# A network of 16 blocks in four interleaved streams on one core: the selective-scan blocks get their decays in PSUM, C's rows from DRAM beside B's, and an earlier input projection of the next batch

## The chip, the cores and the metric

The kernel runs on 1 core of a Trainium2 chip. The metric is the device time of one launch in microseconds (us), the median of several runs of the same program.

## The reference, cut to what matters

The reference is a network of 16 blocks, one after another, on `x` of 8 batches x 256 tokens x 128 channels. Two of them are selective scans (state-space blocks): the first block (`L0_scan`) and the ninth (`L2_scan`). Each normalises its input and computes, per batch:

```
xc, z   = split(x @ W_in)              # 256 channels each; L2: causal conv of 4 taps and SiLU on xc
low,B,C = split(xc @ W_xproj)          # 64, 16 and 16 columns
delta   = softplus(low @ W_dt + b_dt)  # L0: clipped to 0.001 .. 0.1
for n in 16 states, for every channel d, along the tokens t:
    h[t] = decay_n[t] * h[t-1] + delta[t]*xc[t]*B_n[t]
           # decay_n = 1 + A[d,n]*delta (L0) or exp(A[d,n]*delta) (L2)
    y[t] += C_n[t] * h[t]
out = (y + D*xc) * silu(z) @ W_out     # L0 and L2; added to x
```

The other 14 blocks are mixtures of experts, attentions, linear attention, local layers and slot layers. The change leaves what they compute as it is.

## The kernel before, in words

**Streams.** The 8 batches are four streams of two batches. Each stream goes through the 16 blocks in order with its own scratch memory and its own two PSUM banks, called `a` and `b` (128 partitions x 512 f32 each). Stream i begins when stream i-1 has added the result of its first batch of the first block to x (`added`, batch 0), so the streams are in different blocks most of the time and share the five engines.

**How the order of work is set.** Every block (`Part`) writes one generator for each engine: `pe`, `act`, `dve`, `pool`, `sp`. `Core.run` (L513) steps through all generators when the program is built, takes for each engine the piece that by its own list of instruction costs can start first, and emits it. The chip executes that fixed order: an instruction whose semaphore isn't there yet holds up everything behind it on its engine. ScalarE's table loads (L362) are put in by this planner, which lets a function that needs another table wait up to `PATIENCE` = 500 ns longer (L358). Extra matmuls that only keep TensorE's clock up are emitted where a block names a free bank (L533); the scan's inner loop names none.

**The scan block, class `Scan` (L711).** For a batch `bt`:

- TensorE projects the normalised input into bank `a` (`in`, L753). This waits for the skip term of the batch before (`skip`, L751), and in program order it stands behind the output projection (L783) of that batch, which waits for `gated` (L781). ScalarE copies it into `xc` (L803); in L2 a convolution on VectorE (L872) and a SiLU come in between. The convolution writes `h[0]`, which also holds `y`.
- TensorE computes `low` into bank `a` (L759) and B and C, in three copies, into bank `b` (L762). ScalarE copies B out (`b_rows`, L805), then `low` (L806), then a bf16 part of B and C (L807). VectorE forms two more bf16 parts with two subtractions and two casts (`split_dve`, L699, called at L841). Only then (L766) TensorE may overwrite bank `b` with the `dt` projection (L768).
- softplus runs as ScalarE, VectorE, ScalarE, ScalarE, VectorE (L810 to L846); `dx = delta * xc` (L851) ends this prologue.
- B goes to DRAM (`b_out`), and SP loads it back, broadcast to 128 partitions, three states at a time, into two ring buffers (L902): 6 transfers per batch, 5 of 384 KB and one of 128 KB. Batch by batch there are 2 x 4 x 2 = 16 passes over the loop below, 8 in each scan block.

The inner loop over the 16 states `n` has these steps:

1. ScalarE writes `decay[n % 2]` in SBUF, two activations of 128x255 (L824), two states ahead at most (L821). The first columns stay 0.0, from a memset per block (L837).
2. GpSimd (POOL) computes `h[n % 3] = dx * B_n` (`bx`, L900), both inputs in SBUF. It needs the rows of B, and the state n-3 accumulated (L897).
3. VectorE runs the scan over `decay` and `h`, both in SBUF (L857; traced as L405).
4. TensorE spreads C_n over the partitions into bank `b` (`spread`, L773) as a bf16 matmul of K=96.
5. VectorE multiplies h by C_n, which it reads from PSUM (`cmul`, L860).
6. TensorE adds h to bank `a` by a matmul with the identity (`acc`, L776).

After state 15 come the skip term (L863), the gate with `silu(z)` (L867), the output projection (L783) and the addition to x (L870).

Helpers record most instructions under one line: L326 is a matmul, L370 an activation, L392 a VectorE `tensor_tensor`, L397 `tensor_scalar`, L401 `scalar_tensor_tensor`, L405 the scan, L410 a copy or cast, L426 a memset, L460 a GpSimd `tensor_tensor`, L466 an indirect DMA, L480 a DMA from SP.

## Time and profile before

| | us |
|---|---|
| median of 3 runs | 3739.61 |
| the runs | 3732.49, 3739.61, 3739.84 |
| the profiled execution, time | 3741.74 |
| the profiled execution, span of the core | 3740.4 |
| TensorE busy in the span | 3130.3 |
| VectorE busy | 2584.6 |
| ScalarE busy | 2196.5 |
| GpSimd busy | 1512.7 |

The profile is of one execution, 1.3 us longer than its span. A busy engine is one that executes an instruction; a VectorE or GpSimd instruction that is held up after it has started counts as busy and shows a longer duration. The scan blocks lie in two stretches: the first from 48 us to some 450 us, with a remainder until 600 us, the second from 2050 us to 2650 us.

### The profile page before, as it was taken

The numbers are of one execution on the slowest core, as the hardware profiler recorded it, in microseconds if no ns is written. First come the engines' busy times: TensorE is split into PE (matmuls) and PEld (weight loads), VectorE is DVE, ScalarE is ACT, GpSimd is POOL, SyncE is SP. The second block draws the span as 40 slices with busy tenths as digits, with TensorE's granted clock in tenths as the row PEclk, the third lists the DMA queues.
The fourth block names the chain that finished last, engine by engine and source line by source line (L and its number), as shares of the span: only waits on it lengthen the run. The fifth ranks groups of instructions, "written<-read, shape, count | busy, mean of one in ns | idle before, by whom it ended". The sixth has DMA issues, their size and how long they took to land.

```text
span 3740.4 us, 53498 instructions
## 1 busy us (share of the span) xinstructions
PE 3130.3 (84%) x18885; PEld 1842.4 (49%) x19000; DVE 2584.6 (69%) x6180; ACT 2196.5 (59%) x4819; POOL 1512.7 (40%) x1308
## 2 busy tenths in 40 slices
PE   3677697989889999889899877879888888889866
PEld 1244284747544555445555433547465756534422
DVE  3879977474888777667777889976654455556522
ACT  2444445243565777567677664856486756767633
POOL 2545555443455553214655665663303321112100
PEclk9789999999999999999999988999999999999855
DMA  5122142223100010220100011344423543232110
GB/s 210 44 78 65 45 128 76 77 59 90 56 23 1 1 31 8 73 50 14 49 1 10 15 37 36 106 115 122 110 67 106 157 134 92 62 83 51 36 25 5
DMA packets 193604, 238.34 MB, mean 64 GB/s; under 512 B 36984, under 2 KB 154168, under 8 KB 191288
## 3 DMA queue, kind: packets, MB, share of 16 engines
q1 hardware_dynamic: 169016, 157.43, 14.9%
q0 software_dynamic: 24320, 77.47, 6.8%
q8 instruction: 151, 2.47, 0.3%
q14 instruction: 117, 0.96, 0.1%
HBM read 183.61 MB, written 53.74 MB: 63 GB/s over the span
## 4 chain that ended last, share of the span: by engine, by line
PE 35%; DVE 15%; ACT 11%; POOL 5%; issue 4%; SPq 2%; DMA 1%; DVEq 0%; POOLq 0%; ACTq 0%
PE psum L326 31%; ACT scratch L370 7%; DVE scratch L392 6%; PE psum L342 4%; POOL scratch L460 3%; ACT L362 3%; DVE scratch L414 3%; DVE scratch L405 2%; SPq L480 2%; DVE scratch L410 1%; DVE scratch L397 1%; DVE scratch L401 1%; POOL scratch L466 1%; DVE scratch L418 1%; ACT w_early L370 1%
## 5 line engine op out<-in xcount | busy, mean ns | idle before, releaser
L370 ACT ACTIVATE scratch<-psum 128x512 f32<-128x512 f32 (+7 forms) x1812 | 842.7, 494 | 804.2 <-PE psum L326 643.5
L326 PE MATMUL psum<-scratch 128*128 128x128 f32 (+16 forms) x8016 | 935.2, 323 | 123.2 <-ACT scratch L370 40.2
L460 POOL TENSOR_TENSOR scratch<-scratch 128x512 f32<-128x512 f32 (+3 forms) x536 | 706.3, 1331 | 668.5 <-PE psum L326 228.1
L370 ACT ACTIVATE scratch<-scratch 128x255 f32<-128x255 f32 (+11 forms) x1368 | 623.5, 480 | 552.6 <-DVE scratch L405 246.7
L326 PEld LDWEIGHTS psum<-scratch 128*32 128x32 f32 (+9 forms) x8016 | 592.6, 147 | 478.6 <-issue 212.0
L326 PE MATMUL psum<-scratch,w_constants 128*128 128x512 f32 (+2 forms) x848 | 454.7, 630 | 25.7 <-ACT scratch L370 18.8
L362 ACT ACT_TABLE_LOAD x333 | 427.2, 1283 | 31.8 <-PE psum L326 15.0
L405 DVE TENSOR_TENSOR_SCAN scratch<-scratch 128x512 f32<-128x512 f32 x256 | 420.5, 1644 | 16.6 <-POOL scratch L460 13.9
L392 DVE TENSOR_TENSOR scratch<-scratch,psum 128x512 f32<-128x512 f32 (+2 forms) x532 | 309.0, 586 | 138.6 <-PE psum L326 94.7
L342 PE MATMUL psum<-w_constants,scratch 128*128 128x128 f32 (+3 forms) x1880 | 326.2, 294 | 85.8 <-POOL scratch L460 37.2
L326 PE MATMUL psum<-scratch,w_early 128*128 128x512 f32 (+12 forms) x912 | 297.7, 466 | 74.4 <-DVE scratch L392 47.8
L414 DVE TENSOR_REDUCE scratch<-psum 128x2 f32<-128x512 f32 (+2 forms) x336 | 224.6, 676 | 162.5 <-PE psum L326 160.0
L342 PEld LDWEIGHTS psum<-w_constants,scratch 128*128 128x128 f32 (+3 forms) x1880 | 222.6, 144 | 219.1 <-issue 69.7
L392 DVE TENSOR_TENSOR scratch<-psum,scratch 128x512 f32<-128x512 f32 (+4 forms) x456 | 213.1, 474 | 125.0 <-ACT scratch L370 93.5
L466 POOL DMA_INDIRECT scratch<-L_experts_rows_dram,scratch x112 | 119.8, 1070 | 418.6 <-PE psum L326 304.0
L326 PE MATMUL psum<-w_local,scratch 128*128 128x512 f32 (+3 forms) x608 | 257.1, 529 | 20.6 <-DVE scratch L410 10.2
L326 PE MATMUL psum<-scratch,w_local 128*128 128x128 f32 (+6 forms) x1064 | 261.7, 378 | 12.7 <-ACT scratch L370 5.2
L460 POOL TENSOR_TENSOR scratch<-scratch,xpos 128x512 f32<-128x512 f32 x128 | 175.3, 1373 | 209.2 <-DVE scratch L392 207.1
L392 DVE TENSOR_TENSOR scratch<-scratch 128x32 f32<-128x32 f32 (+12 forms) x488 | 212.9, 442 | 61.4 <-ACT scratch L370 51.1
L326 PE MATMUL psum<-scratch,bf_masks 96*128 96x256 bf16 (+4 forms) x480 | 120.2, 286 | 136.4 <-DVE scratch L392 127.0
L326 PEld LDWEIGHTS psum<-scratch,w_early 128*128 128x128 f32 (+6 forms) x912 | 131.3, 180 | 196.4 <-DVE scratch L392 79.7
L460 POOL TENSOR_TENSOR scratch<-scratch,bf_masks 128x512 f32<-128x512 f32 x64 | 76.0, 1189 | 357.8 <-ACT scratch L370 357.5
(106 smaller groups left out, 4219.9 us busy)
## 6 DMA issues: line engine op xcount, KB each, us to landing
scratch<-b_out SPq DMA_DIRECT2D x80, 384.0 KB
slots_out<-scratch SPq DMA_DIRECT2D x112, 128.0 KB, 2.4
q_stack<-scratch SPq DMA_DIRECT2D x72, 192.0 KB, 2.8
scratch<-q_out SPq DMA_DIRECT2D x96, 96.0 KB
scratch<-slots_in SPq DMA_DIRECT2D x16, 512.0 KB
q_out<-scratch SPq DMA_DIRECT2D x40, 192.0 KB, 2.9
scratch<-slots_in SPq DMA_DIRECT2D x16, 448.0 KB
scratch<-q_stack SPq DMA_DIRECT2D x24, 288.0 KB
```

Of the source, the lines that this page charges most:

```text
L326: return self.engine.matmul(out, lhsT, rhs, start=start, stop=stop, **kw)
L342: return self.engine.transpose(out, src, ident)
L362: self.engine.add_instruction(mybir.InstLoadActFuncSet(name=self.nc.get_next_instruction_name(), act_func_set_id=self.table))
L370: return self.engine.activation(out, src, function, **kw)
L392: return self.engine.tensor_tensor(out, a, b, op)
L397: return self.engine.tensor_scalar(out, src, *args)
L401: return self.engine.scalar_tensor_tensor(out, a, scalar, b, *args)
L405: return self.engine.tensor_tensor_scan(out, a, b, *args)
L414: return self.engine.tensor_reduce(out, src, axis, op, **kw)
L460: return self.engine.tensor_tensor(out, a, b, op)
L466: return self.engine.indirect_dma_start(out, out_offset, src, in_offset)
L480: return self.engine.dma_start(out, src)
```

## The change

In both scan blocks:

- The decays go to PSUM bank `b`, as one buffer where there were two in SBUF. Decay n now waits for the scan of state n-1. The two zeros in front (one per half) are written by a small activation per batch; the memsets go.
- C isn't spread by TensorE any more. B and C are written to DRAM together, interleaved by state, and loaded back as two rows per state (B_n, C_n) of 256 KB each time, in four ring buffers: 16 transfers per batch. A buffer is refilled after `cmul` of the state that used it; the third load of a batch waits for `dt`. `cmul` reads C_n from the ring, in SBUF.
- The three copies of B and C, their three bf16 parts, and the four VectorE instructions for them go. `low`, B and C come from one product of 96 columns (two matmuls), copied out by one activation; the `dt` projection waits for that copy alone.
- The input projection of batch 1 (and in L2 its convolution, which now writes `h[2]`) is begun behind the skip term of batch 0, ahead of the output projection.

The attention block's `maxes` semaphores are renamed; nothing else of it changes.

```diff
-    return {"w_in": p[w_in], "w_rank": k_tiles(p[w_xproj][:, :p[w_dt].shape[0]]),
-            "w_bc": k_tiles(np.tile(p[w_xproj][:, p[w_dt].shape[0]:], (1, 3))), "w_dt": p[w_dt], "b_dt": as_cols(p[b_dt]),
+    rank = p[w_dt].shape[0]
+    low, b, c = np.split(p[w_xproj], [rank, (rank + p[w_xproj].shape[1]) // 2], axis=1)
+    b_and_c = np.stack([b, c], 2).reshape(b.shape[0], -1)
+    return {"w_in": p[w_in], "w_x": k_tiles(np.concatenate([low, b_and_c], 1)), "w_dt": p[w_dt], "b_dt": as_cols(p[b_dt]),
...
-        end, self.used = self.used, mark
-        self.b_rows = self.take(T, parts=N)
         self.used = mark
-        rings = [self.take(self.READ, T)]
-        assert self.used >= end
-        self.decay, self.h = ([self.take(D, T) for _ in range(n)] for n in (2, 3))
-        mark = self.used
-        self.low, self.rest = self.take(T, parts=self.rank), self.take(T)
-        self.used = mark
-        self.rings = rings + [self.take(self.READ, T)]
-        self.bc = self.take_bf16(T, parts=3 * 2 * N)
+        self.rings = [self.take(2, T) for _ in range(self.RINGS)]
+        end, self.used = self.used, mark + 4 * T
+        self.low_bc = self.take(T, parts=self.rank + 2 * N)
+        self.low, self.b_and_c = self.low_bc[0:self.rank], self.low_bc[self.rank:]
+        self.used = end
+        self.h = [self.take(D, T) for _ in range(3)]
         self.A = self.take(D, N)
         self.A2, self.B2 = v2(self.a, T), v2(self.b, T)
+        self.decay = self.B2
...
-            e.wait_ge(*(yield self["normed", "x"] if bt == 0 else self["skip", bt - 1]))
+            if bt == 0:
+                e.wait_ge(*(yield self["normed", "x"]))
+                self.pe_in(e, bt)
+            e.wait_ge(*(yield self["xc", bt]))
             for d in range(D):
-                last = e.matmul(self.A2[:, d, :], w["w_in"][:, d * P:(d + 1) * P], xb)
-            last.then_inc(*self.post("in", bt))
-            e.wait_ge(*(yield self["xc", bt]))
+                last = e.matmul(self.a[0:self.rank + 2 * N, 0:T], w["w_x"][:, d * (rank + 2 * N):(d + 1) * (rank + 2 * N)], self.xc[:, d, :],
+                                start=(d == 0), stop=(d == D - 1))
+            last.then_inc(*self.post("low_bc", bt))
+            e.wait_ge(*(yield self["low", bt]))
             if bt:
                 e.wait_ge(*(yield self["added", bt - 1]))
             for d in range(D):
-                e.matmul(self.a[0:rank, 0:T], w["w_rank"][:, d * rank:(d + 1) * rank], self.xc[:, d, :],
-                         start=(d == 0), stop=(d == D - 1))
-            for d in range(D):
-                last = e.matmul(self.b[0:6 * N, 0:T], w["w_bc"][:, d * 6 * N:(d + 1) * 6 * N], self.xc[:, d, :],
-                                start=(d == 0), stop=(d == D - 1))
-            last.then_inc(*self.post("rank_bc", bt))
-            e.wait_ge(*(yield self["low", bt]))
-            e.wait_ge(*(yield self["parts", bt]))
-            for d in range(D):
                 last = e.matmul(self.B2[:, d, :], w["w_dt"][:, d * P:(d + 1) * P], self.low)
             last.then_inc(*self.post("dt", bt))
-            for n in range(N + 1):
-                if n < N:
-                    e.wait_ge(*(yield self["softplus", "delta_raw", bt] if n == 0 else self["cmul", bt, n - 1]))
-                    e.matmul(self.b[:, 0:T], over(self.m["row_of_32"][:, N + n:N + n + 1], [6 * N, P]), self.bc).then_inc(*self.post("spread", bt, n))
-                if n:
-                    e.wait_ge(*(yield self["cmul", bt, n - 1]))
-                    e.matmul(self.a, self.c["ident"], self.h[(n - 1) % 3].rearrange("p a b -> p (a b)"), start=(n == 1),
-                             stop=(n == N)).then_inc(*self.post("acc", bt, n - 1))
+            for n in range(N):
+                e.wait_ge(*(yield self["cmul", bt, n]))
+                e.matmul(self.a, self.c["ident"], self.h[n % 3].rearrange("p a b -> p (a b)"), start=(n == 0),
+                         stop=(n == N - 1)).then_inc(*self.post("acc", bt, n))
...
+            if bt + 1 < PER_STREAM:
+                e.wait_ge(*(yield self["skip", bt]))
+                self.pe_in(e, bt + 1)
...
-            e.wait_ge(*(yield self["rank_bc", bt]))
-            e.activation(self.b_rows, self.b[0:N, 0:T], ACT.Copy).then_inc(*self.post("b_rows", bt))
-            e.activation(self.low, self.a[0:self.rank, 0:T], ACT.Copy).then_inc(*self.post("low", bt))
-            yield from split_act(self, e, bt, self["rank_bc", bt], self.b[0:6 * N, 0:T], self.bc)
+            e.wait_ge(*(yield self["low_bc", bt]))
+            e.activation(self.low_bc, self.a[0:self.rank + 2 * N, 0:T], ACT.Copy).then_inc(*self.post("low", bt))
...
-            if bt == 0:
-                e.wait_ge(*(yield self["zeroed"]))
+            e.activation(self.decay[:, :, 0:1], self.delta[:, :, 0:1], ACT.Copy, scale=0.0)
             for n in range(N):
-                if n >= 2:
-                    e.wait_ge(*(yield self["scanned", bt, n - 2]))
+                if n:
+                    e.wait_ge(*(yield self["scanned", bt, n - 1]))
                 yield None, ACT.Exp if self.a_is_exp else ACT.Identity
                 for d in range(D):
-                    last = e.activation(self.decay[n % 2][:, d, 1:T], self.delta[:, d, 1:T],
+                    last = e.activation(self.decay[:, d, 1:T], self.delta[:, d, 1:T],
...
-        for a in self.decay:
-            last = e.memset(a, 0.0)
-        last.then_inc(*self.post("zeroed"))
         for bt in range(PER_STREAM):
-            if self.conv:
+            if self.conv and bt == 0:
                 yield from self.convolve(e, bt)
-            yield from split_dve(self, e, bt, self.b[0:6 * N, 0:T], self.bc, self.rest)
...
-                flat, a = h.rearrange("p a b -> p (a b)"), self.decay[n % 2].rearrange("p a b -> p (a b)")
+                flat, r = h.rearrange("p a b -> p (a b)"), n % self.RINGS
                 e.wait_ge(*(yield self["decay", bt, n]))
                 e.wait_ge(*(yield self["bx", bt, n]))
-                e.tensor_tensor_scan(flat, a, flat, 0.0, ALU.mult, ALU.add).then_inc(*self.post("scanned", bt, n))
+                e.tensor_tensor_scan(flat, self.b, flat, 0.0, ALU.mult, ALU.add).then_inc(*self.post("scanned", bt, n))
                 e.wait_ge(*(yield self["scanned", bt, n]))
-                e.wait_ge(*(yield self["spread", bt, n]))
-                e.tensor_tensor(h, h, over(self.B2[:, 0:1, :], [P, D, T]), ALU.mult).then_inc(*self.post("cmul", bt, n))
+                e.wait_ge(*(yield self["rows", r, bt, n]))
+                e.tensor_tensor(h, h, over(self.rings[r][:, 1:2, :], [P, D, T]), ALU.mult).then_inc(*self.post("cmul", bt, n))
...
+            if self.conv and bt + 1 < PER_STREAM:
+                yield from self.convolve(e, bt + 1)
...
-                r, i = divmod(n, self.READ)
-                e.wait_ge(*(yield self["rows", r % 2, bt, r]))
+                r = n % self.RINGS
+                e.wait_ge(*(yield self["rows", r, bt, n]))
...
-            rows = self.s.b_out[bt]
-            e.wait_ge(*(yield self["b_rows", bt]))
-            e.dma_start(rows, self.b_rows).then_inc(*self.post_dma("written", bt, "b"))
-            e.wait_ge(*(yield self["written", bt, "b"]))
-            for r in range(-(-self.N // self.READ)):
-                first = r * self.READ
-                count = min(self.READ, self.N - first)
-                if r >= 2:
-                    e.wait_ge(*(yield self["bx", bt, first - self.READ - 1]))
-                elif r:
+            rows = self.s.b_and_c_out[bt]
+            e.wait_ge(*(yield self["low", bt]))
+            e.dma_start(rows, self.b_and_c).then_inc(*self.post_dma("written", bt, "b_and_c"))
+            e.wait_ge(*(yield self["written", bt, "b_and_c"]))
+            for n in range(self.N):
+                if n >= self.RINGS:
+                    e.wait_ge(*(yield self["cmul", bt, n - self.RINGS]))
+                elif n == 2:
                     e.wait_ge(*(yield self["dt", bt]))
-                src = rows[first:first + count].unsqueeze(0).broadcast_to([P, count, TOKENS])
-                e.dma_start(self.rings[r % 2][:, 0:count], src).then_inc(*self.post_dma("rows", r % 2, bt, r))
+                src = rows[2 * n:2 * (n + 1)].unsqueeze(0).broadcast_to([P, 2, TOKENS])
+                e.dma_start(self.rings[n % self.RINGS], src).then_inc(*self.post_dma("rows", n % self.RINGS, bt, n))
```

## Rows read from the trace of the kernel before

**Rows 1.** The page: span, and busy time of each engine.

```profile
span 3740.4 us, 53498 instructions
PE 3130.3 (84%) x18885; PEld 1842.4 (49%) x19000; DVE 2584.6 (69%) x6180; ACT 2196.5 (59%) x4819; POOL 1512.7 (40%) x1308
```

**Rows 2.** Busy time by stretch: stretch, length, then each engine, TensorE's granted clock, DMA share, GB/s.

```profile
48.00:450.00 402.00, 281.13 (x959) 132.26 (x968) 343.12 (x491) 179.75 (x366) 208.93 (x140) 0.89 0.17 55
450.00:600.00 150.00, 139.00 (x847) 101.44 (x850) 112.54 (x177) 67.15 (x118) 87.74 (x78) 0.96 0.34 102
2050.00:2650.00 600.00, 483.49 (x2372) 281.87 (x2387) 512.28 (x911) 382.87 (x796) 353.74 (x256) 0.92 0.25 72
```

**Rows 3.** The same for 50 us of the first stretch.

```profile
150.00:200.00 50.00, 33.81 (x73) 10.81 (x72) 49.47 (x48) 19.58 (x43) 41.05 (x22) 0.81 0.11 34
```

**Rows 4.** The timeline of the state loop of one stream: start, duration.

```profile
162.00 1.64 DVE L405 TENSOR_TENSOR_SCAN scratch<-scratch 128x512 f32<-128x512 f32 x1
163.56 0.65 DVE L392 TENSOR_TENSOR scratch<-scratch,psum 128x512 f32<-128x512 f32 x1
164.14 1.65 DVE L405 TENSOR_TENSOR_SCAN scratch<-scratch 128x512 f32<-128x512 f32 x1
163.67 0.91 ACT L370 ACTIVATE scratch<-scratch 128x255 f32<-128x255 f32 x2 [1.24 <-DVE scratch L405]
148.43 33.46 POOL L460 TENSOR_TENSOR scratch<-scratch 128x512 f32<-128x512 f32 x16
```

**Rows 5.** VectorE's groups by form, 48 to 450 us: count, busy us, mean ns.

```profile
L405 DVE TENSOR_TENSOR_SCAN scratch<-scratch 128x512 f32<-128x512 f32 x107 | 180.8, 1691 | 3.8 <-POOL scratch L460 3.8
L401 DVE SCALAR_TENSOR_TENSOR scratch<-scratch 128x512 f32<-128x512 f32 x14 | 13.6, 968 | 12.2 <-ACT scratch L370 12.2
L392 DVE TENSOR_TENSOR scratch<-scratch 128x512 f32<-128x512 f32 x15 | 12.2, 812 | 2.1 <-ACT scratch L370 1.9
```

**Rows 6.** The same from 2050 to 2650 us.

```profile
L405 DVE TENSOR_TENSOR_SCAN scratch<-scratch 128x512 f32<-128x512 f32 x128 | 203.2, 1588 | 11.0 <-POOL scratch L460 8.3 <-ACT scratch L370 2.7
L401 DVE SCALAR_TENSOR_TENSOR scratch<-scratch 128x512 f32<-128x512 f32 x15 | 12.3, 822 | 7.0 <-ACT scratch L370 6.9
L392 DVE TENSOR_TENSOR scratch<-scratch 128x512 f32<-128x512 f32 x19 | 17.1, 898 | 2.1 <-ACT scratch L370 2.0
```

**Rows 7.** All scans by operands, the whole span: durations min/median/max in ns.

```profile
L405 DVE TENSOR_TENSOR_SCAN scratch<-scratch x256: 1204/1384/7142, 66.6 to 2644.6; 128x512 f32<-128x512 f32 x128
L405 DVE TENSOR_TENSOR_SCAN scratch<-psum,scratch x64: 652/668/691, 787.2 to 1195.9; 128x256 f32<-128x256 f32 x64
```

**Rows 8.** The timeline of the first batch's prologue.

```profile
48.91 1.03 DVE L426 MEMSET scratch<- 128x512 f32 x2 [0.17 <-DVE scratch L392]
51.61 3.92 PE L326 MATMUL psum<-scratch,w_early 128*64 128x256 f32 x8 [0.75 <-ACT scratch L370]
55.57 0.90 ACT L370 ACTIVATE scratch<-psum 16x256 f32<-16x256 f32 x3 [4.01 <-PE psum L326]
56.50 0.42 DVE L392 TENSOR_TENSOR scratch<-psum,scratch 64x256 f32<-64x256 f32 x1 [6.56 <-ACT scratch L370]
57.72 0.28 DVE L410 CAST scratch<-scratch 32x256 bf16<-32x256 f32 x1
66.61 2.20 DVE L405 TENSOR_TENSOR_SCAN scratch<-scratch 128x512 f32<-128x512 f32 x1 [1.51 <-POOL scratch L460]
```

**Rows 9.** TensorE's spreading matmuls, the whole span.

```profile
L326 PE MATMUL psum<-scratch,bf_masks 96*128 96x256 bf16 x256 | 78.3, 307 | 104.3 <-DVE scratch L392 102.1 <-ACT scratch L370 1.3
```

**Rows 10.** ScalarE, 2050 to 2650 us by form, and its timeline at 2602 us.

```profile
L362 ACT ACT_TABLE_LOAD x80 | 102.6, 1283 | 8.1 <-PE psum L326 3.3 <-DVE scratch L405 2.7 <-DVE scratch L392 0.8
2602.94 1.69 ACT L370 ACTIVATE scratch<-scratch 128x255 f32<-128x255 f32 x4
```

**Rows 11.** DMA issues: count, KB each, median us to landing.

```profile
scratch<-b_out SPq DMA_DIRECT2D x80, 384.0 KB
slots_out<-scratch SPq DMA_DIRECT2D x112, 128.0 KB, 2.4
```

21 lines of the change are left out of this document (12 added, 9 removed).

## The prediction

> **What bounds the kernel now.** I read the page first. TensorE is busy for 84% of the span, VectorE for 69% [rows 1], but these are averages over sixteen blocks, and the change touches two. So the next view is busy time by stretch. In the first scan stretch (48 to 450 us) VectorE is busy for 343 of 402 us and TensorE for 281; in the second (2050 to 2650 us) it is 512 and 483 of 600 [rows 2]. VectorE comes first in both, and from 150 to 200 us it is busy for 49.5 of 50 us while TensorE has 33.8 [rows 3]. There the kernel waits for VectorE.
>
> The timeline shows what it does there. Scans start at 162.00 and 164.14: one state takes 2.14 us, a scan of 1.64 and a multiplication by C of 0.65, starts overlapping a little [rows 4]. An undisturbed scan takes 1.21 us (minimum 1204 ns), but the mean of all 128 in the second stretch is 1.588 and of 107 in the first 1.691 [rows 5 to 7]. GpSimd's bx goes on at the same time, 16 in 33.46 us or 2.09 each [rows 4]. The scan and bx both take two inputs from SBUF and hold each other up. The multiplication has one input in PSUM and stays at 0.65. The scans of the GLA block, 256 columns with their first operand in PSUM, are 652 to 691 ns in all 64 cases [rows 7]: never held up, and PSUM costs them nothing, as 256 columns more at the difference (1204 - 652) would give the same 1.2 us.
>
> **The change part by part**, against the profiled execution's 3741.7 us, which is 2.1 us above the median of the runs.
>
> *Decays in PSUM, C in SBUF.* The two VectorE instructions of a state change places. The scan loses its hold-up: 107 x (1.691 - 1.21) = 51 us in the first stretch, 128 x (1.588 - 1.21) = 48 us in the second. The multiplication now has two SBUF inputs. Its nearest rows are VectorE's other instructions of 512 columns with both inputs in SBUF, in the same stretches: 29 that take 25.8 us, 0.89 each, and 34 that take 29.4 us, 0.865 each [rows 5, 6]. Against 0.66 undisturbed, that is 0.23 and 0.20 more: 107 x 0.23 = 25 us and 128 x 0.20 = 26 us. The bounds are nothing (bx fits beside a scan of 1.2 us) and the scan's own 0.48 and 0.38 (51 and 48 us, all given back). I take the rows: VectorE gains 26 and 22 us. The Trainium skill ("SBUF — State Buffer", Who interferes with whom) says that a VectorE instruction with two SBUF inputs contends with a GpSimd instruction that reads SBUF, and that the later one blocks fully; one with a single SBUF input does not. That speaks for the scan and against the multiplication. Rows 5 to 7 agree with both halves.
>
> *No parts, no memsets.* The four VectorE instructions of the split run from 56.50 to 58.00 [rows 8]: 1.5 us, 8 batches per block, 12 us in each. The memsets are 1.03 us in each of 4 streams, 4 us per block. VectorE's sum: 26 + 12 + 4 = 42 us in the first stretch, 22 + 12 + 4 = 38 us in the second.
>
> *The prologue.* Eight matmul instructions of 3.92 us for low, B and C become four, 2.0 us less; three copies of 0.90 us become one, about 0.5 less; the split's 1.5 us go from the chain ahead of dt [rows 8]. That is 4 us from each batch's chain. The early input projection takes the gate, the output projection and their handovers from between the two batches of a stream, some 2 us, 8 times (an estimate; no row of mine has that chain).
>
> *Spreading.* 256 matmuls of 0.307 us go, 78 us of TensorE [rows 9]. TensorE mostly waits for VectorE in the loop, so I count them only from 450 to 600 us, where it is busy for 139 of 150 us [rows 2]: some 22 of the states, with their weight loads some 5 us. Elsewhere they are covered by VectorE; if that cover went, they would be a gain.
>
> *One decay buffer.* Now the decay of n+1 begins when scan n ends and its two activations take 0.91 us [rows 4]. The chain of a stream on its own is scan 1.21, decay 0.91, two handovers of some 0.04: 2.2 us per state, against 2.14 now. So **where one stream scans alone, nothing is gained in the loop**; the multiplication and any hold-up of it lie beside the decay. The gain needs a second stream or other work for VectorE in that gap. No row has an activation that writes PSUM; I take the 0.45 us that one takes now. The low bound is 0.30, a copy out of PSUM (three in 0.90 [rows 8]); as far upwards is 0.60; the ends move the chain by 0.3 us per state. The activation for the zeros, one per batch, costs at most another 0.45 each, 7 us of ScalarE beside VectorE's work.
>
> *Transfers.* B's rows, 80 x 384 KB and 16 smaller ones, become 256 of 256 KB: 64 MB for 32 [rows 11]. In the first stretch DMA runs at 0.17 of its capacity with 55 GB/s [rows 2], so twice the rows fit. SP issues 160 more and waits for the multiplication of n-4. A refill then has until bx of n: about three periods, 6.4 us, less the 1.3 us of bx. 128 KB land in 2.4 us [rows 11]; for 256 KB I estimate 3.2. Covered by 2 us, unless SP stands at another block's wait.
>
> **The sum.** A stretch does not shrink by all that VectorE is spared, since single-stream phases don't. I take half: 21 us in the first, plus 6 us for the first batch of stream 0 and the shorter handover to the next stream (nothing covers these), 27 us. In the second 19 us, less 8 us for ScalarE, see below: 11 us. With 5 us between: 27 + 11 + 5 = 43 us. 3741.7 - 43 = 3699, and 3697 against the median.
>
> **The rivals.**
>
> *B, the hold-ups vanish (20%).* If bx starts when a multiplication ends, its undisturbed 1.1 us fit into the scan's 1.2, and nothing waits. Then VectorE also keeps the 25 + 26 us. The full saving is 42 + 38 + 51 = 131 us; with three quarters on the path 98 us, 3642. For it: in a dense run GpSimd is always queued up behind VectorE [rows 4]. Against it: bx often comes late, released by the accumulation.
>
> *C, the wait moves (13%).* The multiplication inherits the scan's whole hold-up and single streams run at 2.2 us per state. Only the splits and memsets are left, 2 x 16 us, half of them covered, and the first batch's 6 us, against my 8 us for ScalarE and 0.06 us for each of some 120 states: 3741.7 - (16 + 6 - 8 - 7) = 3735, 3733 against the median, within 8.
>
> *D, slower by table loads (12%).* In the second stretch the decays are exponentials between other blocks' functions: 80 table loads there, 1.28 us each [rows 10]. Now two states' decays go out together, 4 activations in 1.69 us [rows 10], under one load. With one buffer that can't be; each state needs ScalarE anew. Every visit that is parted costs two loads, 2.57 us, on the chain scan, decay, scan. It decides above 17 such visits, 43 / 2.57. With 30 parted it costs 77 us against the 51 that I have without my allowance of 8: 3741.7 - 51 + 77 = 3768, 3766 against the median. For it: ScalarE is busy for 383 of 600 us there. Against it: in the first block the decay is no table function, and most decays go out singly already. The Trainium skill ("ScalarE: Activation LUTs", What ACT_TABLE_LOAD costs) adds a drain of about 1.38 us to each load. By that the 30 visits would cost 160 us and the time would be 3851; but in this trace the next activation stands right behind the 1.28 us, so the row decides.
>
> *E, late rows (4%).* If SP, in its fixed order, is held by another block in one load out of four, some 60 waits of 1 us bring 3697 + 60 = 3757.
>
> *F, the scan is held up all the same (3%).* The scan's second input and its output are in SBUF; were that enough, only the multiplication's 51 us would come on top: 3741.7 - 43 + 51 = 3750, 3748 against the median. The 64 scans of GLA speak against it.
>
> **How the numbers follow.** The forecast case has 48%, 3655 to 3722 by its bounds (half of VectorE's saving more or less). With B, C, D, E and F that is 100%. The range reaches down through most of B, to 3625, and up through C to 3748; D, most of E and F, and the tail of B, lie outside. A measurement of this kernel can tell about 0.2%, 7.5 us, from no change. Faster: 46% of the forecast, 20% of B, 6% of C: 0.72. Same: 2% of the forecast, 5% of C, 2% of F: 0.09. Slower: D, E, 2% of C, 1% of F: 0.19. The order in which the program is built shifts in all blocks, which alone can move the time by some us either way; the range has room for that.
>
> **What would show it.** The scans from PSUM at 1.21 us, none above 1.3; the multiplication at 0.80 to 0.95 on average (B: under 0.72, C: above 1.0); VectorE busy for some 80 to 90 us less over the span; TensorE for some 100 less; the dense run at 2.2 us per state with VectorE waiting for ScalarE. Stream 1's first projection some 6 us earlier. In the second stretch ScalarE's table loads at 80 to 90 (D: over 110). No wait of GpSimd for rows longer than 1 us in sum per batch. I am wrong if the first stretch doesn't end 20 us earlier, or if scans of over 1.3 us remain.

## The result, and the profile after the change

The changed kernel takes 3699.6 us (median of 4 runs, 3692.0 to 3705.2) against 3739.7 us (4 runs, 3732.5 to 3747.5): a ratio of 0.9892, with a 95% interval of 0.9867 to 0.9916. The forecast was 3697 us. The profiled execution took 3695.5 us, 1.3 us beyond its span. The page of the kernel after, span and busy time [rows 1]:

```profile
span 3694.2 us, 53129 instructions
PE 3122.3 (85%) x18672; PEld 1841.3 (50%) x18672; DVE 2531.0 (69%) x6100; ACT 2211.5 (60%) x4826; POOL 1438.5 (39%) x1308
```

VectorE is busy for 54 us less, TensorE for only 8 us less. The sum of my forecast was nearly right, so the interesting question is whether the 40 us come from where it put them. First the instructions themselves. VectorE's scan and multiplication in the kernel after, from 48 to 450 us and then from 2050 to 2650 us, by form [rows 5, 6]; the third group of the second fence is the decays, now written to PSUM, the fourth the table loads [rows 10]:

```profile
L406 DVE TENSOR_TENSOR_SCAN scratch<-psum,scratch 128x512 f32<-128x512 f32 x112 | 135.3, 1212 | 13.4 <-POOL scratch L461 10.7 <-ACT psum L371 2.2
L393 DVE TENSOR_TENSOR scratch<-scratch 128x512 f32<-128x512 f32 x128 | 126.8, 996 | 3.3 <-ACT scratch L371 2.2
```

```profile
L406 DVE TENSOR_TENSOR_SCAN scratch<-psum,scratch 128x512 f32<-128x512 f32 x123 | 148.7, 1211 | 29.6 <-ACT psum L371 18.6 <-POOL scratch L461 10.9
L393 DVE TENSOR_TENSOR scratch<-scratch 128x512 f32<-128x512 f32 x140 | 132.7, 952 | 3.7 <-ACT scratch L371 2.8
L371 ACT ACTIVATE psum<-scratch 128x255 f32<-128x255 f32 x246 | 106.7, 467 | 108.6 <-DVE scratch L406 105.4 <-PE psum L327 2.6
L363 ACT ACT_TABLE_LOAD x67 | 86.0, 1283 | 5.5 <-PE psum L327 2.5 <-DVE scratch L406 1.9
```

The scan fell from 1691 and 1588 ns to 1212 and 1211 ns; its slowest case, next fence, is 1226 ns. The multiplication, 0.65 us before, is now 0.95 to 1.0 us (its group holds 16 or 17 others too, of dx and of the gate). The hold-up has changed its instruction, and about a third of it is gone.

Over the whole span the account reads: the scans took 256 x 1.644 = 420.5 us and now take 309.4, 111 less. The multiplications between SBUF tiles were 60 with 47.5 us and are 316 with 296.9 us; what was added is 249.4 us for 256, or 0.974 each, where the PSUM form took 0.67, so 78 us come back. That leaves 33 us, and the splits (64 instructions, 28.4 us) and memsets (7.8) make it 70. The 54 that the page shows are 16 fewer. Most of that lies in instructions that the change leaves alone and that have two SBUF inputs, 11 us more in sum: the 128 of another block that read `xpos` took 115.1 us and take 123.2.

Next, all scans by operands in the kernel after (durations min/median/max in ns, first and last start), up to 700 us and from 2000 us:

```profile
L406 DVE TENSOR_TENSOR_SCAN scratch<-psum,scratch x128: 1185/1210/1225, 62.4 to 516.8; 128x512 f32<-128x512 f32 x128
L406 DVE TENSOR_TENSOR_SCAN scratch<-psum,scratch x128: 1172/1210/1226, 2070.0 to 2665.5; 128x512 f32<-128x512 f32 x128
```

and the same two of the kernel before:

```profile
L405 DVE TENSOR_TENSOR_SCAN scratch<-scratch x128: 1204/1506/7142, 66.6 to 592.5; 128x512 f32<-128x512 f32 x128
L405 DVE TENSOR_TENSOR_SCAN scratch<-scratch x128: 1204/1237/5492, 2055.2 to 2644.6; 128x512 f32<-128x512 f32 x128
```

The last scan of the first block starts 76 us earlier (592.5 to 516.8). The last scan of the second block starts 21 us *later*, and its first already 15 us later. So by 2055 us the lead is gone. Two weight loads, which can only go out once all four streams have left the seventh and the eleventh block, mark the slowest stream's way. SyncE's issues in the kernel before, then after (start us, us):

```profile
1823.36 0.38 SPq L480 DMA_DIRECT2D w_experts<-L_experts_dram  x1
3075.45 0.44 SPq L480 DMA_DIRECT2D w_early<-L_slots_dram  x1
```

```profile
1843.75 0.38 SPq L481 DMA_DIRECT2D w_experts<-L_experts_dram  x1
3071.11 0.37 SPq L481 DMA_DIRECT2D w_early<-L_slots_dram  x1
```

The slowest stream is 20 us *behind* its own time of before at 1823 us, 21 us behind at the end of the second scan block, 4 us ahead at 3075 us, and 46 us ahead at the end. Where does a lead of 76 us go? Busy time by stretch, before and then after (columns as in [rows 2]):

```profile
2650.00:3740.40 1090.40, 904.00 (x6574) 539.67 (x6634) 560.74 (x1656) 678.45 (x1228) 200.20 (x191) 0.88 0.29 77
```

```profile
600.00:2050.00 1450.00, 1299.19 (x7874) 772.38 (x7875) 1017.17 (x2778) 864.48 (x2250) 632.31 (x611) 0.95 0.13 37
2650.00:3694.20 1044.20, 902.27 (x6711) 550.40 (x6711) 567.12 (x1658) 699.18 (x1261) 217.42 (x206) 0.92 0.31 83
```

From 600 to 2050 us TensorE is busy for 1299 of 1450 us, 90%: a block that arrives early there may have to wait for TensorE instead. Its granted clock in this stretch is 0.95; in the kernel before it was 0.97. And behind 2650 us both kernels have about the same work, 904 and 902 us of TensorE by the records (60 of the kernel before's matmuls have none there, 6574 to 6634 weight loads), but the kernel after does it in 1044 us and the one before in 1090. The 46 us by which the spans differ all appear in a part without a scan block. Counted from the last scan, the kernel after makes up 67 us there (21 behind, 46 ahead): 25 of them by 3071 us and 42 behind it.

What differs at the end is how the four streams come in. SyncE's writes of the output, kernel before and then kernel after (start us, us from there to the end of the last, count):

```profile
3511.19 0.38 SPq L480 DMA_DIRECT2D out_dram<-x  x1
3545.81 47.77 SPq L480 DMA_DIRECT2D out_dram<-x  x2
3737.90 0.38 SPq L480 DMA_DIRECT2D out_dram<-x  x1
```

```profile
3488.82 39.21 SPq L481 DMA_DIRECT2D out_dram<-x  x2
3650.76 41.34 SPq L481 DMA_DIRECT2D out_dram<-x  x2
```

Before, three streams are done by 3593.6 and the fourth works alone for 144 us; after, the last one is alone for 41 us. The last 240 us of before have a mean granted clock of 0.64, the last 194 us of after 0.77:

```profile
3500.00:3740.40 240.40, 167.05 (x801) 76.40 (x810) 80.40 (x247) 90.80 (x169) 23.07 (x20) 0.64 0.10 23
```

```profile
3500.00:3694.20 194.20, 150.79 (x853) 69.53 (x850) 80.17 (x242) 91.05 (x177) 27.86 (x23) 0.77 0.12 27
```

So the traces alone offer two theories. **Theory 1**: the scans became cheaper by their place, and the end is earlier because of it. **Theory 2**: the instruction changes bring little, and the order that the planner happened to write for the last blocks brings the rest. The experiments take the instructions first, then the order. They ran on other chips, on which the kernel before takes 3829 to 3844 us, 2.4 to 2.8% more than above; comparisons below are therefore within one chip, or between two on which the kernel before takes the same time.

### The profile page after: what moved, and what is told of

It is laid out like the page before. It is cut to its first block and busy times, and to the rows that moved or that the text cites. A ratio compares the mean times of both kernels' runs of the same rounds, so it can differ in the third digit from the quotient of the medians.

```text
span 3694.2 us, 53129 instructions
## 1 busy us (share of the span) xinstructions
PE 3122.3 (85%) x18672; PEld 1841.3 (50%) x18672; DVE 2531.0 (69%) x6100; ACT 2211.5 (60%) x4826; POOL 1438.5 (39%) x1308
## 5 line engine op out<-in xcount | busy, mean ns | idle before, releaser
L371 ACT ACTIVATE scratch<-psum 128x512 f32<-128x512 f32 (+5 forms) x1780 | 834.0, 496 | 800.8 <-PE psum L327 659.7
L327 PE MATMUL psum<-scratch 128*32 128x128 f32 (+14 forms) x8016 | 941.5, 322 | 105.8 <-ACT scratch L371 39.3
L461 POOL TENSOR_TENSOR scratch<-scratch 128x512 f32<-128x512 f32 (+3 forms) x536 | 641.6, 1209 | 699.3 <-DVE scratch L423 240.8
L371 ACT ACTIVATE scratch<-scratch 128x512 f32<-128x512 f32 (+8 forms) x856 | 396.3, 469 | 228.5 <-DVE scratch L393 142.9
L393 DVE TENSOR_TENSOR scratch<-scratch 128x512 f32<-128x512 f32 (+11 forms) x728 | 448.4, 622 | 68.8 <-ACT scratch L371 56.1
L343 PE MATMUL psum<-w_constants,scratch 128*128 128x128 f32 (+2 forms) x1880 | 329.8, 297 | 77.0 <-POOL scratch L461 45.4
L371 ACT ACTIVATE psum<-scratch 128x255 f32<-128x255 f32 (+1 forms) x528 | 224.0, 458 | 272.8 <-DVE scratch L406 258.9
L406 DVE TENSOR_TENSOR_SCAN scratch<-psum,scratch 128x512 f32<-128x512 f32 (+1 forms) x320 | 349.6, 1104 | 50.9 <-ACT psum L371 23.2
L343 PEld LDWEIGHTS psum<-w_constants,scratch 128*128 128x128 f32 (+2 forms) x1880 | 226.8, 146 | 211.2 <-issue 69.3
L327 PE MATMUL psum<-scratch,w_early 128*128 128x512 f32 (+10 forms) x848 | 279.8, 465 | 61.7 <-DVE scratch L393 45.2
L327 PE MATMUL psum<-scratch,w_local 128*128 128x128 f32 (+5 forms) x1064 | 265.8, 385 | 7.7 <-ACT scratch L371 5.5
```

Source lines behind the costliest of these rows:

```text
L327: return self.engine.matmul(out, lhsT, rhs, start=start, stop=stop, **kw)
L343: return self.engine.transpose(out, src, ident)
L371: return self.engine.activation(out, src, function, **kw)
L393: return self.engine.tensor_tensor(out, a, b, op)
L406: return self.engine.tensor_tensor_scan(out, a, b, *args)
L461: return self.engine.tensor_tensor(out, a, b, op)
```

## The experiments

### The two scan blocks alone

The network is cut to its two scan blocks, without the weights that the full kernel loads later, for the kernel before, for the kernel after, and for two variants of the latter.

```diff
-            for group, block, how in NETWORK:
+            for group, block, how in NETWORK[0:1] + NETWORK[8:9]:
...
-            for g, after in LATER.items():
+            for g, after in ():
```

The kernel before, cut:

> The kernel before with its two scan blocks alone, one behind the other (the other 14 blocks are left out). Theory (VectorE's hold-ups, the split and the prologue are what the change saves): this is the base, about 48 us of loading and 256 states at 2.14 to 2.3 us, some 650 to 750 us. The rival (the gain of the whole kernel is only another packing of the other blocks at the end) says nothing of this run alone.

The kernel after, cut:

> The changed kernel with its two scan blocks alone. Theory: 40 to 90 us less than the same cut of the kernel before (VectorE spared 80 us, prologues 4 us shorter each). Rival (packing elsewhere): within 15 us of it.

A second buffer for the decay, in SBUF, used alternately with the one in PSUM:

```diff
-        self.decay = self.B2
+        self.decay = [self.B2, self.take(D, T)]
...
-                if n:
-                    e.wait_ge(*(yield self["scanned", bt, n - 1]))
+                if n >= 2:
+                    e.wait_ge(*(yield self["scanned", bt, n - 2]))
...
-                e.tensor_tensor_scan(flat, self.b, flat, 0.0, ALU.mult, ALU.add)
+                e.tensor_tensor_scan(flat, self.decay[n % 2].rearrange("p a b -> p (a b)"), flat, 0.0, ALU.mult, ALU.add)
```

> The changed kernel's two scan blocks alone, with a second decay buffer in SBUF beside the one in PSUM, used in turn. If the single buffer is what a lone stream waits for (2.2 us per state), this is 10 to 40 us shorter than the cut of the changed kernel, although every second scan has two SBUF inputs again and can be held up. If hold-ups dominate, it is the same or up to 30 us longer.

One buffer for the decay, but in SBUF (so both VectorE instructions of a state have two SBUF inputs):

```diff
-        self.decay = self.B2
+        self.decay = self.take(D, T)
...
-                e.tensor_tensor_scan(flat, self.b, flat, 0.0, ALU.mult, ALU.add)
+                e.tensor_tensor_scan(flat, self.decay.rearrange("p a b -> p (a b)"), flat, 0.0, ALU.mult, ALU.add)
```

> The changed kernel's two scan blocks alone, with its one decay buffer in SBUF instead of PSUM, so that scan and multiplication both have two SBUF inputs. If the place of the decays is what frees the scan, the scans go back to 1.5 us or more and the whole is 60 us or more longer than the cut of the changed kernel. If the shorter prologue and the rows of C bring the gain, it is within 20 us of it.

Measured, on one chip (one execution each, which does for differences of 80 us and more):

| cut kernel | us | scan, mean ns | multiplication, mean ns |
|---|---|---|---|
| before | 845.6 | 1599 | 665 |
| after | 709.5 | 1210 | 782 |
| after, second decay buffer in SBUF | 828.4 | 1209 and 1680 | 1017 |
| after, its one decay buffer in SBUF | 929.3 | 1954 | 851 |

The rows behind the table, by form, of the scans and of the changed kernel's multiplication. First the cut kernel before:

```profile
L405 DVE TENSOR_TENSOR_SCAN scratch<-scratch 128x512 f32<-128x512 f32 x256 | 408.6, 1599 | 12.0 <-POOL scratch L460 12.0
```

The cut kernel after:

```profile
L406 DVE TENSOR_TENSOR_SCAN scratch<-psum,scratch 128x512 f32<-128x512 f32 x256 | 309.2, 1210 | 13.7 <-ACT psum L371 7.3 <-POOL scratch L461 5.6
L393 DVE TENSOR_TENSOR scratch<-scratch 128x512 f32<-128x512 f32 x288 | 223.4, 782 | 6.7 <-ACT scratch L371 4.8
```

With the second buffer in SBUF:

```profile
L406 DVE TENSOR_TENSOR_SCAN scratch<-scratch 128x512 f32<-128x512 f32 x128 | 214.9, 1680 | 0.0
```

With the one buffer in SBUF:

```profile
L406 DVE TENSOR_TENSOR_SCAN scratch<-scratch 128x512 f32<-128x512 f32 x256 | 499.7, 1954 | 16.3 <-ACT scratch L371 9.1 <-POOL scratch L461 7.1
```

Three things follow. The place of the decay, and nothing else in the change, frees the scan: with the same code and the decay in SBUF it is held for 0.74 us on average, and the time is 220 us longer, worse even than before by 84 us. The planner writes another order for this kernel, and TensorE's mean granted clock is 0.63 in it against 0.84, but VectorE is busy for 213 us more (797.0 against 584.2), which is nearly all of the 220. A second buffer in SBUF doesn't pay: whatever the longer look-ahead gives, every other scan is held for 0.47 us, the multiplications behind them too, and the kernel is 119 us slower. (A second buffer in PSUM wasn't tried: bank `a` accumulates and bank `b` is the one in use.) And with only scan blocks in the mix the change is worth 136 us, 16%. The mechanism of the forecast is shown. The sizes that I had expected were too small: 650 to 750 us for the cut kernel before, 40 to 90 us for the change, and at most 30 us of loss for the second buffer.

Why the multiplication pays only about 0.12 us here and 0.31 in the full kernel is seen in the timeline of the cut kernel after, around 250 us:

```profile
249.35 0.66 DVE L393 TENSOR_TENSOR scratch<-scratch 128x512 f32<-128x512 f32 x1
249.39 1.75 POOL L461 TENSOR_TENSOR scratch<-scratch 128x512 f32<-128x512 f32 x1
249.94 1.21 DVE L406 TENSOR_TENSOR_SCAN scratch<-psum,scratch 128x512 f32<-128x512 f32 x1
251.66 1.21 DVE L406 TENSOR_TENSOR_SCAN scratch<-psum,scratch 128x512 f32<-128x512 f32 x1
```

One state takes 1.72 us (249.94, 251.66), the multiplications are undisturbed at 0.66, and GpSimd's bx goes in the same beat. But bx does not start when the multiplication ends: it starts 0.03 us behind the multiplication's start and lasts 1.75 us. The length fits a hold-up through the multiplication's 0.66 us and then 1.09 us of work beside the scan. So in this beat GpSimd pays the whole hold-up and VectorE none. That is what my rival B wanted for VectorE, by another way than its paragraph gave. In the full kernel this beat occurs too, from 157.71 us:

```profile
157.71 1.21 DVE L406 TENSOR_TENSOR_SCAN scratch<-psum,scratch 128x512 f32<-128x512 f32 x1
159.43 1.21 DVE L406 TENSOR_TENSOR_SCAN scratch<-psum,scratch 128x512 f32<-128x512 f32 x1
```

but where other work comes in between it breaks, and held multiplications stand in the same timeline, of 1.76 us and, once, of 5.48:

```profile
204.95 1.76 DVE L393 TENSOR_TENSOR scratch<-scratch 128x512 f32<-128x512 f32 x1
233.82 5.48 DVE L393 TENSOR_TENSOR scratch<-scratch 128x512 f32<-128x512 f32 x1
233.83 4.91 POOL L461 TENSOR_TENSOR scratch<-scratch 128x512 f32<-128x512 f32 x4
```

The second one is held over four bx in a row, all of which start after it. A hold-up is not limited to one instruction of GpSimd's.

### The first four blocks

How much of the first block's gain outlives the blocks behind it? The network is cut to its first four blocks, without later weights.

```diff
-            for group, block, how in NETWORK:
+            for group, block, how in NETWORK[:4]:
```

> The first four blocks of the kernel before alone (scan, experts, linear attention, experts; the other 12 left out). It is the base of the next. VectorE leads in the scan, TensorE in the three blocks behind it; some 900 to 1100 us.

> The first four blocks of the changed kernel alone. The first scan block by itself should save half of the 136 us that the two save alone, 68 us. If the blocks behind it, bound by TensorE, take most of that back because they can't start their own work faster, the four blocks are 15 to 40 us shorter than those of the kernel before. If the gain passes through whole, 55 us or more. If it is lost already among mixed work, under 15 us.

Measured, one execution each: 1053.7 us before, 1017.6 after, 36 us less, within the 15 to 40 that I had expected. The last scan starts at 521.0 instead of 605.3 us, 84 us earlier; so 48 of 84 us are given back to three blocks in which TensorE has the longer share (it is busy for 76% of this cut kernel's span, VectorE for 61%). The lead is real, the end of this network is 36 us earlier, and more than half of the lead is lost within three blocks. (Here, too, the end is a tail: the last stream is alone for 77 us before and for 9 after, so the 36 are no pure price of the state.)

### The order written by the planner

The planner lets a ScalarE function that needs another table wait up to `PATIENCE` = 500 ns longer. A tenth more or less changes no instruction's work, only the order, in all blocks. This shows what an order is worth.

```diff
-PATIENCE = 500
+PATIENCE = 450
```

For the kernel before:

> The kernel before, with the planner's constant for table loads at 450 instead of 500: the same instructions in another order, nothing that the change touches. It measures what an order alone moves. If order alone is worth little, within 0.4% of the kernel before (ratio 0.996 to 1.004); if the gain of the change could be luck of the order, 1% or more either way.

For the kernel after:

> The changed kernel with the same constant at 450. If the change brings its 1.1% by its mechanism, ratio 0.985 to 0.993 against the kernel before, whatever the order. If its 1.1% is luck of the order, anything from 0.985 to 1.01.

The kernel after with 550:

> The changed kernel with the planner's constant at 550: its instructions in a third order. If the change brings its gain whatever the order, ratio 0.985 to 0.995. If orders differ by as much as the gain, outside of that, up to 1.005.

And the kernel after as it is:

> The changed kernel itself, unedited, beside the others of this study. If its gain holds from chip to chip, ratio 0.985 to 0.993 against the kernel before; it is the base for the late input and for the other orders. If part of the 1.1% hangs on the chip's speed, 0.993 to 1.0.

The second decay buffer of above in the full network, in the order of 450:

> The changed kernel at 450 with a second decay buffer in SBUF, used in turn with the one in PSUM. To be read against the changed kernel at 450. If the single buffer costs in the whole network (ScalarE late for the next decay, table loads that can't be shared), 10 to 30 us faster than that; if other streams cover it, within 8 us; if the hold-up of every second scan costs more, 10 to 20 us slower.

| kernel, full network | us | against before, 95% interval |
|---|---|---|
| before | 3829.2 to 3829.7 | |
| before, 450 | 3839.0 | 1.0017 (1.0002 to 1.0033) |
| after | 3800.3 | 0.9925 (0.9896 to 0.9954) |
| after, 450 | 3809.6 | 0.9954 (0.9940 to 0.9968) |
| after, 550 | 3806.4 | 0.9931 (0.9902 to 0.9959) |
| after, 450, second decay buffer | 3843.7 | 1.0038 (1.0016 to 1.0059) |

These ran on two chips, on which the kernel before takes the same (3829.2 and 3829.7). Two orders of the kernel before stand at 3829 and 3839, three of the kernel after at 3800 to 3810. So the constant alone moves the time by 0.1 to 0.3%, and in all three orders the kernel after is ahead. The table sets each row against the kernel before at 500. With the same constant on both sides the change is worth 29 us twice: 3829.7 to 3800.3 at 500, and 3839.0 to 3809.6 at 450, 0.77% each. At 450 the two sets of ten runs, on one chip, don't overlap (3804.8 to 3818.3 against 3824.9 to 3850.2). And there the tail is not what differs. The last writes of the output, kernel before at 450 and then kernel after at 450:

```profile
3816.44 30.60 SPq L480 DMA_DIRECT2D out_dram<-x  x2
```

```profile
3790.77 14.77 SPq L481 DMA_DIRECT2D out_dram<-x  x2
```

The last stream is alone for 31 us in the one and for 15 in the other. The kernel before at 450 is the slower of the two orders of the kernel before even so, though in the profile of the order at 500, on the first chip, the last stream is alone for 144 us. So a long tail by itself does not decide the time, and theory 2, put as a matter of the tail alone, doesn't hold at 450. On these chips the change is worth 0.77% like for like, against 1.1% where it was first measured. Against my expectations: the kernel before at 450 and the kernel after at 500 and 550 came out as the theory had it, the kernel after at 450 did not (0.9954, where I had 0.985 to 0.993 against the kernel before at 500). The second buffer costs 34 us at the same constant (I had expected at most 20), with its SBUF scans at 1550 ns; the full network confirms the sign of the cut one, though its order differs too.

### The early input undone

The next batch's input projection and convolution go back behind the output projection; all else stays.

```diff
-            if bt == 0:
-                e.wait_ge(*(yield self["normed", "x"]))
-                self.pe_in(e, bt)
+            e.wait_ge(*(yield self["normed", "x"] if bt == 0 else self["skip", bt - 1]))
+            self.pe_in(e, bt)
...
-            if bt + 1 < PER_STREAM:
-                e.wait_ge(*(yield self["skip", bt]))
-                self.pe_in(e, bt + 1)
...
-            if self.conv and bt == 0:
+            if self.conv:
                 yield from self.convolve(e, bt)
...
-            if self.conv and bt + 1 < PER_STREAM:
-                yield from self.convolve(e, bt + 1)
```

> The changed kernel with the input projection of the second batch put back behind the output projection of the first (and the convolution at the start of the batch). If the early projection is worth its 2 us per stream and block, 2 to 16 us slower than the changed kernel; if it is covered by other streams, within the spread of orders, some 8 us either way.

Measured: 3828.1 us, a ratio of 1.0000 (0.9986 to 1.0014), 28 us slower than the changed kernel on the other chip, where I had expected 2 to 16. By this, without the early input nothing of the gain is left. Before crediting 28 us to one projection, look where they lie. (The traces are of one execution each, of 3818 and 3804 us.) The scans of this kernel from 2000 us:

```profile
L406 DVE TENSOR_TENSOR_SCAN scratch<-psum,scratch x128: 1165/1210/1225, 2014.5 to 2667.2; 128x512 f32<-128x512 f32 x128
```

The same of the unedited kernel after in this study:

```profile
L406 DVE TENSOR_TENSOR_SCAN scratch<-psum,scratch x128: 1172/1210/1225, 2121.0 to 2718.5; 128x512 f32<-128x512 f32 x128
```

With the late input the first block's last scan is 5 us later (528.1 for 522.9), but the second block's is 51 us *ahead*; and then the end is later. SyncE's writes of the output, late input and then the unedited kernel:

```profile
3542.43 54.34 SPq L481 DMA_DIRECT2D out_dram<-x  x2
3668.20 0.38 SPq L481 DMA_DIRECT2D out_dram<-x  x1
3814.26 0.38 SPq L481 DMA_DIRECT2D out_dram<-x  x1
```

```profile
3599.97 40.48 SPq L481 DMA_DIRECT2D out_dram<-x  x2
3759.25 41.32 SPq L481 DMA_DIRECT2D out_dram<-x  x2
```

A stream works alone for 146 us at the end, as in the kernel before, against 41. So an order in which the second scan block is early can end late. What this run shows is that 28 us can hang on the early projection and the order that comes with it, which one edit changed together; it doesn't show that the projection earns them by itself, nor, after the orders at 450, that the tail does. It keeps theory 2 alive in this form: a kernel with all its scans at 1.21 us can end where the kernel before does.

## Why the prediction was right, and where it was not

**Right: the price of the scan.** All 256 scans of the full kernel are below 1.23 us, none above 1.3. The Trainium skill ("SBUF — State Buffer", Who interferes with whom) has it that a second input from PSUM takes a VectorE instruction out of the contention, and the run with the decay back in SBUF shows that this alone does it. Rival F, the scan held all the same, fell.

**Half right: the chain of a lone stream.** Where one stream is alone the bound is mostly scan, decay, scan, with VectorE waiting for ScalarE. I had 2.2 us; the timeline of the kernel after, from 83.99 us, has 2.16 (83.99, 86.15). That "the multiplication and any hold-up of it lie beside the decay" was wrong: a held one of 1.73 us outlasts the decay's 0.87, and that state takes 2.92 us (86.15, 89.07):

```profile
83.99 1.22 DVE L406 TENSOR_TENSOR_SCAN scratch<-psum,scratch 128x512 f32<-128x512 f32 x1 [0.15 <-ACT psum L371]
85.25 0.87 ACT L371 ACTIVATE psum<-scratch 128x255 f32<-128x255 f32 x2 [1.29 <-DVE scratch L406]
86.15 1.22 DVE L406 TENSOR_TENSOR_SCAN scratch<-psum,scratch 128x512 f32<-128x512 f32 x1 [0.21 <-ACT psum L371]
87.41 1.73 DVE L393 TENSOR_TENSOR scratch<-scratch 128x512 f32<-128x512 f32 x1
89.07 1.21 DVE L406 TENSOR_TENSOR_SCAN scratch<-psum,scratch 128x512 f32<-128x512 f32 x1
```

Of the 15 steps of this first batch, 5 take 2.8 us or more, and the mean is 2.40 us. In the kernel before it is 2.40 too, not the 2.14 of my one pair of starts. So "nothing is gained in the loop" where one stream is alone came true, at another level than I had.

My "dense run at 2.2 us per state with VectorE waiting for ScalarE" was too general, though: with two streams a state takes 1.72.

**Right: the prologue.** The timeline of the first batch in the kernel after [rows 8]: four matmuls in 2.02 us for eight in 3.92, one copy of 0.38 for three of 0.90, and the first scan is 4.2 us earlier, for the 4 that I had.

```profile
51.44 2.02 PE L327 MATMUL psum<-scratch,w_early 128*96 128x256 f32 x4 [0.75 <-ACT scratch L371]
53.50 0.38 ACT L371 ACTIVATE scratch<-psum 96x256 f32<-96x256 f32 x1 [2.11 <-PE psum L327]
62.42 1.22 DVE L406 TENSOR_TENSOR_SCAN scratch<-psum,scratch 128x512 f32<-128x512 f32 x1 [1.50 <-POOL scratch L461]
```

Stream 1's first projection starts 5.0 us earlier, for the 6 forecast (kernel before, then after):

```profile
117.85 2.04 PE L326 MATMUL psum<-scratch,w_early 128*128 128x256 f32 x4 [0.20 <-DVE scratch L392]
112.87 1.53 PE L327 MATMUL psum<-scratch,w_early 128*128 128x256 f32 x4 [3.63 <-DVE scratch L393]
```

**Right: the transfers.** The waits of GpSimd for rows, over the whole span of the kernel after (us, times, longest), are 10.3 us in 16 batches:

```profile
POOL scratch L461 <- DMA scratch<-b_and_c_out: 10.3, 22, 0.9
```

That is under 1 us per batch, and rival E fell. DMA's share in the first 600 us rose from 0.28 to 0.38.

**Right: table loads.** In the second stretch there were 67 for 80 [rows 10], where I had 80 to 90 and rival D over 110, although each state now needs ScalarE anew. Part of the fall is the window, since the block now ends later: from 2050 us to the block's last scan it is 71 for 79, and to 2700 us 84 for 81. The two scan blocks alone have 30 in both kernels. So rival D fell, and no run shows a need for my 8 us of allowance. Over the whole span loads rose, 333 to 356, and 18 of these 23 lie in the first 600 us; as the scan blocks alone need no more, I put them down to the order, which is not shown.

**Wrong: the multiplication's price.** "0.23 and 0.20 more" was 0.34 and 0.29 (0.996 and 0.952 against 0.66), 78 us over the span instead of 51. Of the 80 us in my sum ("80 to 90 us less" among the signs) this takes 27; the scans gave 12 more than I had, the splits 4 more, and unchanged instructions took back some 16, which leaves the 54. The price was too low because of a share, and the traces count it: of the 63 instructions from which I took it, 23 found an instruction of GpSimd's at work when they started (or starting within 20 ns); of the 268 of the multiplication's group in the same stretches of the kernel after, 150 did. Those took 1.21 and 1.20 us on average, the others 0.68 in both. Ten of the 150 lasted over 2 us, held over up to four bx, and make 29 of the 84 us that the group spends above 0.66. For these the prediction's "the later one blocks fully" is no account either: in the row at 233.82 us the bx start later and go first. By the marks that I had set, the full kernel lies between forecast (0.80 to 0.95) and rival C (above 1.0); the cut kernel lies just under the forecast on average (0.78, with 32 others in its group) and at rival B in its dense run (0.66). One instruction has all these prices, by its company.

**Wrong: "TensorE for some 100 less".** The page says 8, and it can't be read as it stands. Before, 18885 matmuls stand to 19000 weight loads [rows 1]; after, 18672 to 18672. The 115 matmuls without a record are all among those that only keep the clock up: 533 matmuls (172.1 us) to 648 weight loads before, 640 to 640 after. At 0.32 us each they are some 37 us that the page of before lacks. What was to go is gone: 78 us of spreading and 19 of the prologue's matmuls (64, 19.2 us). Against it, the groups with as many matmuls as before took 33 us longer in sum, at a mean granted clock of 0.925 for 0.930; a group of 384 went from 634 to 659 ns. The rest is in how matmuls overlap, which I didn't resolve. The planner did not fill the gap with more clock keeping, 640 for 648.

**Wrong: the sum's parts, 27 + 11 + 5.** The step that failed is "A stretch does not shrink by all that VectorE is spared ... I take half", together with the silent assumption that what a stretch gains reaches the end. The first block ends 76 us earlier, not 27. That is more than all of the 42 us that I had VectorE spared there with the 6 of the prologue, so something else, the order for one, has a part in it as well (not shown). It is given back in the blocks behind: 48 of 84 us by the fourth block in the cut network, all of it and 20 us more by 1823 us in the full one. That TensorE takes it is argued from its 90%, not tested; waiting for TensorE alone would leave the stream level with its time of before. That it falls 20 us behind could come from the order or from the lower granted clock (0.95 for 0.97); no run separates them. The second block, for which I had 11 us, ends 21 us later. All 46 us appear behind 2650 us, where the kernel after makes up 67, with a tail of 41 us in place of 144. So the predicted time was met with parts that were not: gains and losses that I hadn't named cancelled, and that the sum came within 3 us was luck. The early input's "some 2 us, 8 times" was not shown either way.

**Wrong on paper: the case's bounds.** "3655 to 3722" with "half of VectorE's saving more or less" does not follow: half of 80 us is 40, which gives 3657 to 3737, and the multiplication's own bounds, halved, give some 3672 to 3721. The measured 3700 lies inside all of them.

**Open.** How much of the 1.1% is the cheaper state and how much the order, the packing of the last streams included. For the first speak the cut networks, -136 and -36 us, three orders of the kernel after that all beat the kernel before, and the same 29 us at both constants, at 450 with short tails on both sides; for the second the late input at 1.0000 and the milestones, which have the changed kernel behind at 1844 and 2665 us. No kernel was run that holds the order fixed while the instructions change, which would settle it. None of the versions run was faster than the changed kernel.

## What to carry to other kernels

Of two consecutive VectorE instructions that run beside GpSimd, give the PSUM operand to the longer one: the hold-up then falls on the shorter, and the long one may even shelter all of GpSimd's work. Price a hold-up by its company: count how often the instruction will find GpSimd at work (here 56% of the instructions did, where those that I had priced it by had 37%), and let the range reach beyond one instruction of the other engine, since a hold-up went on over four. Compare versions with the planner's constants equal on both sides. Where a planner interleaves streams, a gain in one block is a gain at the end only if the blocks behind it wait for that block and the last streams still come in together: look at when each stream delivers before crediting a step with the time.

## What the runs showed of the hardware that was not expected

- VectorE and GpSimd fall into a common beat: 1.72 us per state, in which bx starts with the multiplication, lasts 1.75 us instead of the 1.26 of a free one, and VectorE's two instructions are not held. A scan with two SBUF inputs alone takes 1.60 to 1.95 us on average in the same company.
- A VectorE instruction with two SBUF inputs can be held over several GpSimd instructions that start after it: 5.48 us for a multiplication over four bx (kernel after, 233.82 us), 7.14 us for a scan over five, four of them started after it (kernel before, 245.85 us).
- An activation of 128x255 from SBUF takes 467 ns written to PSUM (cut kernel after, 512 of them) and 499 ns written to SBUF (cut kernel before, 512), 6% less. I had assumed no difference.
- GpSimd gains as well: bx falls from 1912 to 1544 ns in the cut kernels, 93 us over 256 of them. The hold-up is paid on both sides.
- The same kernel before takes 3740 us on one chip and 3829 to 3844 on others, with a mean granted clock of 0.92 to 0.93 on the first and, for full kernels, 0.90 to 0.92 on the others. A difference of 2.4% between chips is twice what the whole change is worth.
